# The second weights of all sixteen experts are kept on chip in a vision tower with a mixture of experts

## The chip, the cores and the metric

The kernel runs on one core of one Trainium2 chip. The metric is the device time of a run in microseconds. Three runs of the kernel before gave 906.76, 907.35 and 907.6 us; their median is 907.35 us.

## The reference, cut to what matters

```
tok   = concat(class, patches(x) @ W.T + b) * pos         # 128 images x 65 tokens x 128, x is 128 x 3 x 224 x 224
h     = tok + sigmoid([window_attention(ln(tok)), ln(tok)] @ W_c)
z     = layer_norm(ln(h), g, b)                           # the block's input is ln(h)
gate  = softmax((z @ router_w + router_b) / 0.7)          # 16 experts, the best 2 are kept
ey    = silu(z @ ew1[e] + eb1[e]) @ ew2[e] + eb2[e]       # ew1: 16 x 128 x 512, ew2: 16 x 512 x 128
moe   = sum over the 2 experts of gate * ey  +  0.25 * shared(z)
out   = h + ln(h) + moe + silu(layer_norm(moe) @ ff_w1 + ff_b1) @ ff_w2 + ff_b2
```

All of it is float32. The expert part has 8320 tokens with two experts each, 16640 rows.

## The kernel before, in words

Each engine runs its own program, and semaphores tie them together. There are three stages.

The first stage takes 16 groups of 512 tokens. SP loads images into two halves of one large buffer, `region` (`xb[0]` and `xb[1]`, 14336 columns each), VectorE and ScalarE move them into the patch buffers `xf` and `xlast`, and TensorE multiplies them with the patch weights `wp`; attention, routing and layer norms of the group before are woven in. GpSimd scatters each token's normalised row twice into the DRAM buffer `z_rows`, sorted by expert. In the last group the image loads stop, and SP uses the free halves of `region` for what the next stage needs: the shared expert's weights, tokens of earlier groups (`load_ht`, the first `HT_LOW`, which is 6, at once and six more when `xb[1]` is free), and first and second weights of experts 0 to 3 (`w1b`, `w2b`, lines 485 and 486).

The second stage takes 80 tiles of 256 rows, each of one expert. Tiles 0 to 15 are the first tile of experts 0 to 15; for the others a table `ejc`, made on chip at the end of the first stage, holds the expert's number. The first four tiles and the last five steps are written out, and the rest is a loop of four tiles per turn. A step `j` on TensorE (`step2`) is: transpose tile `j+1` (`t_in`, line 1615), the up-projection of tile `j` (`up`, line 1626: 4 column blocks x 3 terms of split float32, 12 matmuls), and the down-projection of tile `j-1` (`down`, line 1637: 2 row halves x 4 blocks, each matmul run as two passes, 16 in all). ScalarE takes the transpose out of PSUM (line 788) and applies silu (line 798) with the expert's bias, whose address it gets by reading `ejc` into a register (line 794). VectorE splits rows and first weights into high and low parts (lines 1274 to 1279 and 1223 to 1225), and adds the expert's second bias to the down-projection (line 1268). GpSimd scatters the result rows (line 916).

SP feeds this stage. For tile `j` it reads the tile's row into a register and loads the rows (`expert_rows`, line 514), then reads the expert's number and loads 256 KB of first weights (line 506) and 256 KB of second weights (line 508). All three have four buffers in a ring. Every fourth tile it also loads a residual (line 542). The order of these loads is the order of the program. Before the loop SP zeroes the tails of `z_rows` (line 419), loads the first four tiles' rows, the third stage's weights (line 534) and two more token loads (line 475).

The third stage gathers the two results of each token, adds the shared expert, and runs the last feed-forward block.

Of the kernel before, what the change touches and what calls it, by code (L numbers as in the profile page):

```python
# [28 lines left out]
P = 128  # L29
D = 128  # L30
# [5 lines left out]
TILES = PATCH_TILES + 1  # L36
GT = 4
GTOK = GT * P
GIMG = GTOK // SEQ
GROUPS = PATCH_TILES // GT  # L40
TOKENS = TILES * P
E, DH, DS = 16, 512, 256
EC, SC = DH // P, DS // P
TOPK = 2
# [11 lines left out]
MAIN = 21  # L56
# [11 lines left out]
N_LOADS = 18  # L68
FILL, EARLY = 7, 12
SP_TAILS = 12  # L70
assert EARLY % 2 == 0 and EARLY + 4 == GROUPS
# [41 lines left out]
def build(nc, consts, x, tok_w, tok_b, cls_tok, pos, w_c, ln_g, ln_b, r_w, r_b, ew1, eb1, ew2, eb2,  # L113
          sw1, sb1, sw2, sb2, f_g, f_b, fw1, fb1, fw2, fb2, out):
    with ExitStack() as ctx:
        def sb(name, shape, dt=F32):
            return ctx.enter_context(nc.sbuf_tensor(name, shape, dt))

        def sem(name):
            return ctx.enter_context(nc.semaphore(name))  # L120
# [24 lines left out]

        wp = sb("wp", [P, MAIN, D])
        wc = sb("wc", [P, 2, D])
# [11 lines left out]
        XZ = XCOLS // 4  # L159
        region = sb("region", [P, 2 * XCOLS])  # L160
        xb = [region[:, u * XCOLS:(u + 1) * XCOLS] for u in range(2)]
# [6 lines left out]
        def carve(n):  # L168
            carved[0] += n
            assert carved[0] <= 2 * XCOLS  # L170
            return region[:, carved[0] - n:carved[0]]
# [3 lines left out]
        sw2_t = carve(SC * D).rearrange("p (c d) -> p c d", c=SC)  # L175
        ht3 = [carve(GTOK) for _ in range(2)]
        assert carved[0] <= XCOLS
        shared_with_stage3 = carved[0]
        w1b = [carve(W) for _ in range(4)]
        w2b = [carve(W).rearrange("p (c d) -> p c d", c=EC) for _ in range(4)]  # L180
        eh_at = carved[0]
        ehT = [carve(EC * EROWS).rearrange("p (c r) -> p c r", c=EC) for _ in range(2)]
        zin = [carve(EH * ZW).rearrange("p (h d) -> p h d", h=EH) for _ in range(4)]
        h2T = [carve(EROWS) for _ in range(2)]
        yout = [carve(EH * D).rearrange("p (h d) -> p h d", h=EH) for _ in range(2)]
        fw1_t = carve(DH)
        fw2_t = carve(EC * D).rearrange("p (c d) -> p c d", c=EC)
        r_at = carved[0]
        r_res = carve(TILES * D)
        HT_LOW = (XCOLS - r_at) // GTOK  # L190
        sh_res = carve(TILES * D)


        carved[0] = shared_with_stage3
        moe = [carve(GT * D).rearrange("p (t d) -> p t d", t=GT) for _ in range(2)]
        z4 = carve(GT * D).rearrange("p (t d) -> p t d", t=GT)
        h4T = carve(GTOK)
        ffs = carve(EC * GTOK).rearrange("p (c r) -> p c r", c=EC)
        assert carved[0] <= eh_at
        carved[0] = eh_at  # L200
        gat = [carve(GT * TOPK * D).rearrange("p (t k d) -> p t k d", t=GT, k=TOPK) for _ in range(2)]
        assert 2 * GT * TOPK * D <= 2 * EC * EROWS + 4 * EH * ZW + 2 * EROWS + 2 * EH * D

# [4 lines left out]

        xf = sb("xf", [P, QUADS * 4 * HTOK])
        xquad = [xf[:, u * 4 * HTOK:(u + 1) * 4 * HTOK].rearrange("p (q t j) -> p q t j", q=2, j=2) for u in range(QUADS)]  # L210
        xlast = sb("xlast", [P, HTOK])
        eb2_rows = xf[:, 0:E * D]
        shs = [xf[:, E * D + u * SC * GTOK:E * D + (u + 1) * SC * GTOK].rearrange("p (c r) -> p c r", c=SC) for u in range(2)]
        wparts = sb("wparts", [P, 2 * DH + 2 * DS], F32R)
# [116 lines left out]
        w1_loaded = [sem(f"w1_loaded{u}") for u in range(4)]  # L331
        w2_loaded = [sem(f"w2_loaded{u}") for u in range(4)]
        zin_loaded = [sem(f"zin_loaded{u}") for u in range(4)]
# [37 lines left out]
        def one(body, g):  # L371
            body(g, g % 2, g // 2)
# [33 lines left out]
        def units_before(g, u):  # L406

            return g * (HALVES * UNITS) + u * UNITS
# [17 lines left out]
        def _(sp):  # L426
# [52 lines left out]
            for dst, src in ((sw1_t, sw1), (sw2_t, sw2.rearrange("(c p) d -> p c d", p=P)),  # L479
                             (sbq[:, :], sb2.partition_broadcast(P))):  # L480
                sp.dma_start(dst, src).then_inc(sh_loaded, 16)
            for i in range(HT_LOW):
                load_ht(i)
            for j in range(FIRST):
                sp.dma_start(w1b[j], ew1[j]).then_inc(w1_loaded[j], 16)
                sp.dma_start(w2b[j], ew2[j].rearrange("(c p) d -> p c d", p=P)).then_inc(w2_loaded[j], 16)
            one(stores, GROUPS - 3)
            sp.wait_ge(memset_done, 1)

            for s in range(2, SPARE_TILES):  # L490
                at = SPARE_AT + s * EROWS
                sp.dma_start(z_rows[at:at + EROWS].rearrange("(p h) d -> p h d", p=P), zsrc).then_inc(spare_zeroed, 16)
            sp.wait_ge(xact_ready, units_before(GROUPS, 0))
            for i in range(HT_LOW, EARLY):
                load_ht(i)
            one(stores, GROUPS - 2)
            sp.wait_ge(xunit_used, units_before(GROUPS, 0))
# [5 lines left out]
            def expert_weights(j, n):  # L503
                ex = sp.value_load(ejc[0:1, bass.ds(j, 1)], min_val=0, max_val=E - 1)
                sp.wait_ge(w1l_ready, j - 3)
                sp.dma_start(w1b[n % 4], ew1[bass.ds(ex, 1)].rearrange("o d h -> d (o h)")).then_inc(w1_loaded[n % 4], 16)
                sp.wait_ge(down_done, j - 3)
                sp.dma_start(w2b[n % 4], ew2[bass.ds(ex, 1)].rearrange("o (c p) d -> p (o c) d", p=P))\
                  .then_inc(w2_loaded[n % 4], 16)

# [14 lines left out]
            for j in range(FIRST):  # L525
                sp.dma_start(zin[j], z_rows[j * CAP:j * CAP + EROWS].rearrange("(p h) d -> p h d", p=P))\
                  .then_inc(zin_loaded[j], 16)
            zero_tails(sp, FIRST, SP_TAILS)

            sp.wait_ge(r_free, 16 * (GROUPS + 1))  # L530
# [887 lines left out]
        def _(pe):  # L1418
# [210 lines left out]

            def down(j, n, h):  # L1630
                pe.wait_ge(w2_loaded[n % 4], h * 16 + 16)
                if n > 1:
                    pe.wait_ge(yout_ready, j - 1)
                pe.wait_ge(eh_ready, j * EC + EC)
                for i in range(EH):
                    for c in range(EC):
                        ins = pe.matmul(bank[5 + n % 2][:, i * P:(i + 1) * P], ehT[n % 2][:, c, i * P:(i + 1) * P],  # L1637
                                        w2b[n % 4][:, c], start=c == 0, stop=c == EC - 1)
                ins.then_inc(down_done, 1)

            def step2(j, n, h, first=0):

                if not (isinstance(j, int) and j + 1 >= EXPERT_TILES):
                    t_in(j + 1, n + 1, h + (n % 4 + 1) // 4)
                if not (isinstance(j, int) and j >= EXPERT_TILES):
                    up(j, n, h)
                if n - 1 >= first and not (isinstance(j, int) and j > EXPERT_TILES):
                    down(j - 1, n - 1, h - (n % 4 == 0))

            t_in(0, 0, 0)  # L1650
            pe.wait_ge(shr_ready, EARLY)
            for j in range(4):
                step2(j, j, 0)
            with pe.Fori(1, EXPERT_TILES // 4 - 1) as i:
                for n in range(4):
                    step2(i * 4 + n, 4 + n, i)
# [78 lines left out]
```

## Time and profile before

| what | value |
|---|---|
| median of three runs | 907.35 us |
| span of the profiled execution, first to last instruction | 972.0 us |
| first stage, about | 0 to 517 us |
| expert stage, about | 517 to 829 us |
| third stage, about | 829 to 972 us |
| TensorE, weight loads of TensorE, VectorE, ScalarE, GpSimd busy | 92, 82, 70, 62, 45% of the span |
| bytes moved by SP's queue | 166.24 MB |
| mean granted clock of TensorE | 0.975 of full |

The profile is of one execution, with a recording of every instruction and DMA packet. Its span is the only time shown of it, and it is longer than the runs without a recording. PE is TensorE's matmuls, PEld its weight loads, DVE VectorE, ACT ScalarE, POOL GpSimd; SPq is SP's queue, and a name with q (ACTq, PEldq) means instructions that an engine's sequencer handles alone, such as register loads. Stages have different bounds, so the shares over the span say little of any one of them.

### The profile page before, as it was taken

The page shows a single profiled execution, that of the slowest core. Times are in us where ns is not written, and L with a number is a line of the kernel's source. Part 1 is how long each engine was busy: PE and PEld are TensorE (multiplying, and loading weights), DVE is VectorE, ACT ScalarE, POOL GpSimd, SP SyncE. Part 2 cuts the span into 40 slices and gives each one's busy share as a digit, 9 for nine tenths or more (in the row PEclk, how much of TensorE's full clock was granted, in tenths as well). Part 3 has the DMA queues.
Part 4 walks back from the last instruction along what each step waited for, and adds up shares of the span by engine and source line. Part 5 has one row for each costly group of instructions (what it writes and reads, how often), then busy time and mean ns, then how long its engine had stood idle before and what let it go on. Part 6 is the DMA issues. An engine that isn't in the chain of part 4 may idle for free. (4 is left out here: it accounts for less than half of the span.)

```text
span 972.0 us, 22164 instructions
## 1 busy us (share of the span) xinstructions
PE 896.2 (92%) x5920; PEld 801.2 (82%) x5920; DVE 676.2 (70%) x2244; ACT 599.5 (62%) x1064; POOL 438.8 (45%) x374
## 2 busy tenths in 40 slices
PE   2999999989999999999889999999999899789999
PEld 2788888778878888888779889898999899679888
DVE  8377877757877887787556666666676675488884
ACT  3567666656666666777645565555555565477766
POOL 6012554425555545554451445455555464334342
PEclk9999999979999999999879999999999999989999
DMA  9999999977788888767137687777778675334432
GB/s 225 224 221 225 242 247 240 237 205 210 213 228 218 214 216 219 194 216 213 50 105 215 196 227 218 214 219 228 216 224 236 184 221 166 107 82 115 107 103 57
DMA packets 194299, 186.96 MB, mean 192 GB/s; under 512 B 16797, under 2 KB 168698, under 8 KB 194010
## 3 DMA queue, kind: packets, MB, share of 16 engines
q1 hardware_dynamic: 183168, 166.24, 65.2%
q0 software_dynamic: 9376, 19.42, 6.1%
q10 hardware_dynamic: 1722, 0.93, 0.5%
q8 instruction: 12, 0.20, 0.1%
q14 instruction: 21, 0.17, 0.1%
HBM read 150.48 MB, written 36.04 MB: 192 GB/s over the span
## 5 line engine op out<-in xcount | busy, mean ns | idle before, releaser
L1435 PE MATMUL bank<-xf,wp 128*128 128x256 f32 x1280 | 314.0, 394 | 8.4 <-ACT xf L632 5.4
L1435 PEld LDWEIGHTS bank<-xf,wp 128*128 128x128 f32 x1280 | 237.7, 192 | 51.6 <-issue 7.4
L916 POOL DMA_INDIRECT y_tok<-region,dsti x160 | 162.9, 1018 | 164.9 <-DVE region L1268 119.0
L874 POOL TENSOR_TENSOR rstd<-var,neghalf 128x4 f32<-128x4 f32 (+2 forms) x51 | 80.6, 1580 | 287.9 <-DVE var L1030 156.4
L632 ACT ACTIVATE xf<-region 128x1024 f32<-128x1024 f32 x160 | 174.0, 1137 | 18.3 <-DVE region L947 18.3
L890 POOL DMA_INDIRECT z_rows<-z,posg x130 | 157.3, 1210 | 52.5 <-issue 52.2
L798 ACT ACTIVATE region<-bank,cols 128x256 f32<-128x256 f32 x320 | 132.3, 476 | 55.2 <-PE bank L1626 37.2
L1637 PE MATMUL bank<-region 128*128 128x128 f32 x1280 | 156.8, 275 | 1.1 <-DVE region L1268 1.0
L1637 PEld LDWEIGHTS bank<-region 128*128 128x128 f32 x1280 | 150.4, 192 | 1.7 <-issue 1.5
L1626 PE MATMUL bank<-parts 128*128 128x256 f32 x960 | 136.6, 290 | 14.2 <-DVE parts L1279 8.8
L1626 PEld LDWEIGHTS bank<-parts 128*128 128x128 f32 x960 | 119.6, 190 | 25.7 <-issue 19.0
L947 DVE COPY region<-region 32x1792 f32<-32x1792 f32 x96 | 104.8, 1092 | 50.3 <-ACT hT L652 28.9
L788 ACT ACTIVATE region<-bank,cols 128x256 f32<-128x256 f32 x80 | 45.4, 567 | 81.0 <-PE bank L1615 46.5
L1223 DVE CAST parts<-region 128x512 fp32r<-128x512 f32 x80 | 35.4, 443 | 70.9 <-DMA region<-in_L_ffn_ew 56.7
L1684 PE MATMUL bank<-region 128*128 128x128 f32 x520 | 61.7, 277 | 0.0
L1684 PEld LDWEIGHTS bank<-region 128*128 128x128 f32 x520 | 59.4, 192 | 0.9 <-ACT region L819 0.5
L1225 DVE TENSOR_TENSOR parts<-region,parts 128x512 fp32r<-128x512 f32 x80 | 55.6, 694 | 2.8
L1329 DVE SCALAR_TENSOR_TENSOR region<-region,w_all 128x128 f32<-128x128 f32 x130 | 50.3, 446 | 7.6 <-issue 5.3
L1665 PE MATMUL bank<-parts,wparts 128*128 128x512 f32 (+1 forms) x204 | 51.5, 403 | 3.4 <-DVE parts L1368 3.4
L1665 PEld LDWEIGHTS bank<-parts,wparts 128*128 128x128 f32 x204 | 37.5, 195 | 12.0 <-issue 3.6
L834 ACT ACTIVATE region<-region,nmr,rstd 128x128 f32<-128x128 f32 x65 | 26.9, 484 | 30.3 <-DVE nmr L1363 30.3
L819 ACT ACTIVATE region<-bank,cols 128x512 f32<-128x512 f32 (+1 forms) x68 | 40.6, 657 | 3.0 <-PE bank L1665 3.0
(183 smaller groups left out, 1232.3 us busy)
## 6 DMA issues: line engine op xcount, KB each, us to landing
region<-in_x SPq DMA_DIRECT2D x384, 196.0 KB
region<-in_L_ffn_ew SPq DMA_DIRECT2D x160, 256.0 KB
region<-z_rows SPq DMA_DIRECT2D x80, 130.0 KB
region<-y_tok SPq DMA_DIRECT2D x16, 512.0 KB, 3.6
ht_dram<-hT SPq DMA_DIRECT2D x16, 256.0 KB
r_dram<-rr SPq DMA_DIRECT2D x16, 256.0 KB
region<-ht_dram SPq DMA_DIRECT2D x16, 256.0 KB, 5.5
region<-r_dram SPq DMA_DIRECT2D x16, 256.0 KB
```

The lines of the kernel that those rows point to most:

```text
L632: ins = act.activation(xquad[i].rearrange("p q t j -> p t q j"), src[:, :, 4 * i:4 * i + 4].rearrange("p t (q j) -> p t q j", j=2), ACT.Copy)
L798: act.activation(ehT[n % 2][:, c], bank[1 + c][:, 0:EROWS], ACT.Silu, bias=bias[c])\
L874: pool.tensor_tensor(dst, var, neghalf[:, 0:var.shape[1]], ALU.pow).then_inc(ready, 1)
L890: pool.indirect_dma_start(z_rows, bass.IndirectOffsetOnAxis(posg[k][:, n:n + 1], 0), z[k][:, t], None).then_inc(z_free[k], 16)
L916: pool.indirect_dma_start(y_tok, bass.IndirectOffsetOnAxis(dsti[n % 2][:, i:i + 1], 0), yout[n % 2][:, i], None).then_inc(y_free[n % 2], 16)
L947: dve.tensor_copy(dst, src).then_inc(block_moved, 1)
L1225: dve.tensor_tensor(w1l[n % 2], w1b[n % 4], w1h[n % 2], ALU.subtract).then_inc(w1l_ready, 1)
L1435: ins = pe.matmul(out_cols, wp[:, s], cols_in, start=s == 0, stop=s == MAIN - 1)
L1626: ins = pe.matmul(bank[1 + c][:, 0:EROWS], w[n % 2][:, c * P:(c + 1) * P], v[n % 2], start=i == 0, stop=i == len(terms) - 1)
L1637: ins = pe.matmul(bank[5 + n % 2][:, i * P:(i + 1) * P], ehT[n % 2][:, c, i * P:(i + 1) * P], w2b[n % 4][:, c], start=c == 0, stop=c == EC ...
L1665: ins = pe.matmul(dst, w[:, c * P:(c + 1) * P], v[:, 0:nt * P], start=i == 0, stop=i == len(terms) - 1)
L1684: ins = pe.matmul(bank[FFD_BANK[k]][:, t * P:(t + 1) * P], ffs[:, c, t * P:(t + 1) * P], fw2_t[:, c], start=c == 0 and t == 0, stop=c == E ...
```

## The change: what it does

The second weights of all 16 experts get a place of their own in SBUF, `w2all` (16 x 512 columns). They are loaded once: experts 0 to 3 before the last group's end, 4 to 7 when `xb[1]` is free, 8 to 15 after the last table zeroing. SP's loop no longer loads second weights and no longer waits for `down_done`. TensorE reads the expert's number of tile `j-1` into a register in each step, between `t_in` and `up`, and the down-projection addresses `w2all` by that register; for tiles 0 to 15 in the written-out steps the number is known when the program is built. TensorE waits for the three groups of loads by constants. To make room, the patch buffers `xf` and `xlast` and the patch weights `wp` move into one arena with `region`, and the expert stage's smaller buffers move into their part of it. Six token loads (`FIRST_HT` to `EARLY`) no longer wait for `xb[1]`.

```diff
+FIRST_HT = 6
...
-        wp = sb("wp", [P, MAIN, D])
...
-        region = sb("region", [P, 2 * XCOLS])
+        XF, XL, WP = QUADS * 4 * HTOK, HTOK, MAIN * D
+        ARENA = 2 * XCOLS + XF + XL + WP
+        region = sb("region", [P, ARENA])
...
+        r_res = carve(TILES * D)
         assert carved[0] <= XCOLS
-        shared_with_stage3 = carved[0]
+        weights_at = carved[0]
         w1b = [carve(W) for _ in range(4)]
-        w2b = [carve(W).rearrange("p (c d) -> p c d", c=EC) for _ in range(4)]
-        eh_at = carved[0]
+        W2_LOW = (XCOLS - carved[0]) // W
+        w2all = carve(E * W)
+        weights_end = carved[0]
         ehT = [carve(EC * EROWS).rearrange("p (c r) -> p c r", c=EC) for _ in range(2)]
+        h2T = [carve(EROWS) for _ in range(2)]
+        assert carved[0] <= 2 * XCOLS
+        sh_res = carve(TILES * D)
...
+        eb2_rows = carve(E * D)
+        shs = [carve(SC * GTOK).rearrange("p (c r) -> p c r", c=SC) for _ in range(2)]
         zin = [carve(EH * ZW).rearrange("p (h d) -> p h d", h=EH) for _ in range(4)]
...
+        xf = region[:, 2 * XCOLS:2 * XCOLS + XF]
...
-        w2_loaded = [sem(f"w2_loaded{u}") for u in range(4)]
+        w2_low, w2_mid, w2_high = sem("w2_low"), sem("w2_mid"), sem("w2_high")
...
-            for i in range(HT_LOW):
+            def load_w2(lo, hi, done):
+                for e in range(lo, hi):
+                    sp.dma_start(w2all[:, e * W:(e + 1) * W].rearrange("p (c d) -> p c d", c=EC),
+                                 ew2[e].rearrange("(c p) d -> p c d", p=P)).then_inc(done, 16)
+
+            for i in range(FIRST_HT):
                 load_ht(i)
             for j in range(FIRST):
                 sp.dma_start(w1b[j], ew1[j]).then_inc(w1_loaded[j], 16)
-                sp.dma_start(w2b[j], ew2[j].rearrange("(c p) d -> p c d", p=P)).then_inc(w2_loaded[j], 16)
             one(stores, GROUPS - 3)
...
+            for i in range(FIRST_HT, EARLY):
+                load_ht(i)
+            load_w2(0, W2_LOW, w2_low)
+            one(stores, GROUPS - 2)
             sp.wait_ge(xact_ready, units_before(GROUPS, 0))
-            for i in range(HT_LOW, EARLY):
-                load_ht(i)
-            one(stores, GROUPS - 2)
+            load_w2(W2_LOW, 2 * W2_LOW, w2_mid)
             sp.wait_ge(xunit_used, units_before(GROUPS, 0))
...
                 sp.wait_ge(w1l_ready, j - 3)
                 sp.dma_start(w1b[n % 4], ew1[bass.ds(ex, 1)].rearrange("o d h -> d (o h)")).then_inc(w1_loaded[n % 4], 16)
-                sp.wait_ge(down_done, j - 3)
-                sp.dma_start(w2b[n % 4], ew2[bass.ds(ex, 1)].rearrange("o (c p) d -> p (o c) d", p=P))\
-                  .then_inc(w2_loaded[n % 4], 16)
...
             zero_tails(sp, FIRST, SP_TAILS)
+            load_w2(2 * W2_LOW, E, w2_high)
...
-            def down(j, n, h):
-                pe.wait_ge(w2_loaded[n % 4], h * 16 + 16)
+            def down(j, n, ex):
                 if n > 1:
                     pe.wait_ge(yout_ready, j - 1)
                 pe.wait_ge(eh_ready, j * EC + EC)
+                w2 = [w2all[:, bass.ds(ex * W + c * D, D)] for c in range(EC)]
                 for i in range(EH):
                     for c in range(EC):
                         ins = pe.matmul(bank[5 + n % 2][:, i * P:(i + 1) * P], ehT[n % 2][:, c, i * P:(i + 1) * P],
-                                        w2b[n % 4][:, c], start=c == 0, stop=c == EC - 1)
+                                        w2[c], start=c == 0, stop=c == EC - 1)
...
                     t_in(j + 1, n + 1, h + (n % 4 + 1) // 4)
-                if not (isinstance(j, int) and j >= EXPERT_TILES):
+                if n - 1 >= first:
+                    ex = j - 1 if static and j - 1 < E else \
+                        pe.value_load(ejc[0:1, bass.ds(j - 1, 1)], min_val=0, max_val=E - 1)
+                if not (static and j >= EXPERT_TILES):
                     up(j, n, h)
...
             pe.wait_ge(shr_ready, EARLY)
+            pe.wait_ge(w2_low, 16 * W2_LOW)
             for j in range(4):
                 step2(j, j, 0)
+            pe.wait_ge(w2_mid, 16 * W2_LOW)
+            pe.wait_ge(w2_high, 16 * (E - 2 * W2_LOW))
+            pe.wait_ge(tab_ready, 1)
             with pe.Fori(1, EXPERT_TILES // 4 - 1) as i:
```

`W2_LOW` comes out as 4.

## Rows read from the trace of the kernel before

**Rows 1.** The page, part 1: busy us (share) xinstructions of each engine.

```profile
PE 896.2 (92%) x5920; PEld 801.2 (82%) x5920; DVE 676.2 (70%) x2244; ACT 599.5 (62%) x1064; POOL 438.8 (45%) x374
```

**Rows 2.** Weight loads of TensorE in order of time: start, us, count, idle before.

```profile
531.31 1.49 PEld L1626 LDWEIGHTS bank<-parts 128*128 128x128 f32 x12 [0.54 <-issue]
...
823.01 1.50 PEld L1626 LDWEIGHTS bank<-parts 128*128 128x128 f32 x12
```

**Rows 3.** Matmuls of TensorE in order of time, where nothing is late.

```profile
745.95 1.67 PE L1626 MATMUL bank<-parts 128*128 128x256 f32 x12
747.46 1.95 PE L1637 MATMUL bank<-region 128*128 128x128 f32 x16
749.25 0.38 PE L1615 MATMUL bank<-cst,region 128*128 128x128 f32 x2
749.38 1.67 PE L1626 MATMUL bank<-parts 128*128 128x256 f32 x12
```

**Rows 4.** Waits of the expert loop, 531 to 823 us: total, times, longest.

```profile
DVE parts L1223 <- DMA region<-in_L_ffn_ew: 53.9, 42, 3.6
...
PEld bank L1626 <- issue: 19.0, 35, 1.0
...
PE bank L1626 <- DVE parts L1279: 8.5, 26, 0.7
```

**Rows 5.** The same stretch: busy us of each engine, clock, DMA share, GB/s.

```profile
531.30:823.00 291.70, 273.74 (x2247) 259.95 (x2248) 190.71 (x544) 166.19 (x392) 153.18 (x151) 1.00 0.75 214
```

**Rows 6.** What SP itself waited for in that stretch.

```profile
SPq L508 <- remote: 2.2, 4, 1.6
```

**Rows 7.** SP's weight loads: count, ns min/median/max, first and last start.

```profile
L506 SPq DMA_DIRECT2D region<-in_L_ffn_ew x76: 4/318/725, 524.7 to 816.6; - x76
...
L508 SPq DMA_DIRECT2D region<-in_L_ffn_ew x76: 13/396/1010, 525.2 to 817.1; - x76
```

**Rows 8.** SP's queue in order of time, an undisturbed stretch.

```profile
655.16 0.32 SPq L506 DMA_DIRECT2D region<-in_L_ffn_ew  x1
655.58 0.40 SPq L508 DMA_DIRECT2D region<-in_L_ffn_ew  x1
656.92 0.35 SPq L514 DMA_DIRECT2D region<-z_rows  x1
```

**Rows 9.** Register work of ScalarE: count, ns min/median/max, first and last start.

```profile
L794 ACTq FUSED_REGOPS  x152: 42/152/152, 518.8 to 822.0; - x152
L794 ACTq TENSOR_LOAD <-ejc x80: 273/279/497, 518.4 to 821.6; - x80
...
L798 ACTq FUSED_REGOPS  x320: 46/46/51, 519.3 to 826.1; - x160
```

**Rows 10.** Register instructions of TensorE's sequencer at single places (start us).

```profile
L1613 PEldq ALU_OP  x1: 32/32/32, 652.2 to 652.2; - x1
...
L1634 PEldq ALU_OP  x1: 32/32/32, 653.0 to 653.0; - x1
...
L1634 PEldq ALU_OP  x1: 32/32/32, 638.5 to 638.5; - x1
...
L1654 PEldq ALU_OP  x1: 32/32/32, 638.9 to 638.9; - x1
```

**Rows 11.** TensorE's weight loads just after the third of these places.

```profile
653.11 1.49 PEld L1626 LDWEIGHTS bank<-parts 128*128 128x128 f32 x12
```

**Rows 12.** Busy times, clock, DMA share and GB/s, 519 to 531 us.

```profile
519.00:531.00 12.00, 12.00 (x104) 11.71 (x102) 7.80 (x23) 7.86 (x20) 2.11 (x2) 1.00 0.90 256
```

**Rows 13.** Start of the expert loop: SP's queue and VectorE in order of time.

```profile
519.24 0.89 SPq L534 DMA_DIRECT2D region<-in_L_ffn_ff_w  x2
...
524.72 0.35 SPq L506 DMA_DIRECT2D region<-in_L_ffn_ew  x1
...
528.47 0.43 DVE L1223 CAST parts<-region 128x512 fp32r<-128x512 f32 x1 [2.81 <-DMA region<-in_L_ffn_ew]
528.93 0.69 DVE L1225 TENSOR_TENSOR parts<-region,parts 128x512 fp32r<-128x512 f32 x1
```

**Rows 14.** SP's queue in the last group of the first stage.

```profile
449.32 0.50 SPq L498 DMA_DIRECT2D xf<-in_L_ffn_eb  x1
472.67 0.33 SPq L447 DMA_DIRECT2D ht_dram<-hT  x1
```

More of the change, by code:

```diff
@@ L169, in carve @@
             carved[0] += n
-            assert carved[0] <= 2 * XCOLS
+            assert carved[0] <= ARENA
             return region[:, carved[0] - n:carved[0]]
@@ L176, in build @@
         ht3 = [carve(GTOK) for _ in range(2)]
+        r_res = carve(TILES * D)
         assert carved[0] <= XCOLS
-        shared_with_stage3 = carved[0]
+        weights_at = carved[0]
         w1b = [carve(W) for _ in range(4)]
-        w2b = [carve(W).rearrange("p (c d) -> p c d", c=EC) for _ in range(4)]
-        eh_at = carved[0]
+        W2_LOW = (XCOLS - carved[0]) // W
+        w2all = carve(E * W)
+        weights_end = carved[0]
         ehT = [carve(EC * EROWS).rearrange("p (c r) -> p c r", c=EC) for _ in range(2)]
+        h2T = [carve(EROWS) for _ in range(2)]
+        assert carved[0] <= 2 * XCOLS
+        sh_res = carve(TILES * D)
+        assert carved[0] >= 2 * XCOLS
+        eb2_rows = carve(E * D)
+        shs = [carve(SC * GTOK).rearrange("p (c r) -> p c r", c=SC) for _ in range(2)]
         zin = [carve(EH * ZW).rearrange("p (h d) -> p h d", h=EH) for _ in range(4)]
-        h2T = [carve(EROWS) for _ in range(2)]
         yout = [carve(EH * D).rearrange("p (h d) -> p h d", h=EH) for _ in range(2)]
[L186 to L194, printed above, removed]
+        fw1_t = sb("fw1_t", [P, DH])[:, :]
+        fw2_t = sb("fw2_t", [P, EC * D])[:, :].rearrange("p (c d) -> p c d", c=EC)
+        carved[0] = weights_at
         moe = [carve(GT * D).rearrange("p (t d) -> p t d", t=GT) for _ in range(2)]
@@ L198, in build @@
         ffs = carve(EC * GTOK).rearrange("p (c r) -> p c r", c=EC)
-        assert carved[0] <= eh_at
-        carved[0] = eh_at
         gat = [carve(GT * TOPK * D).rearrange("p (t k d) -> p t k d", t=GT, k=TOPK) for _ in range(2)]
-        assert 2 * GT * TOPK * D <= 2 * EC * EROWS + 4 * EH * ZW + 2 * EROWS + 2 * EH * D
+        assert carved[0] <= weights_end
         parts = sb("parts", [P, 4 * W + 4 * EROWS], F32R)
@@ L207, in build @@
         h2h, h2l = ([parts[:, 4 * W + (2 * c + u) * EROWS:4 * W + (2 * c + u + 1) * EROWS] for u in range(2)] for c in range(2))
-        xf = sb("xf", [P, QUADS * 4 * HTOK])
+        xf = region[:, 2 * XCOLS:2 * XCOLS + XF]
         xquad = [xf[:, u * 4 * HTOK:(u + 1) * 4 * HTOK].rearrange("p (q t j) -> p q t j", q=2, j=2) for u in range(QUADS)]
-        xlast = sb("xlast", [P, HTOK])
-        eb2_rows = xf[:, 0:E * D]
-        shs = [xf[:, E * D + u * SC * GTOK:E * D + (u + 1) * SC * GTOK].rearrange("p (c r) -> p c r", c=SC) for u in range(2)]
+        xlast = region[:, 2 * XCOLS + XF:2 * XCOLS + XF + XL]
+        wp = region[:, 2 * XCOLS + XF + XL:ARENA].rearrange("p (s h) -> p s h", s=MAIN)
         wparts = sb("wparts", [P, 2 * DH + 2 * DS], F32R)
@@ L1637, in down @@
                         ins = pe.matmul(bank[5 + n % 2][:, i * P:(i + 1) * P], ehT[n % 2][:, c, i * P:(i + 1) * P],
-                                        w2b[n % 4][:, c], start=c == 0, stop=c == EC - 1)
+                                        w2[c], start=c == 0, stop=c == EC - 1)
                 ins.then_inc(down_done, 1)
             def step2(j, n, h, first=0):
-                if not (isinstance(j, int) and j + 1 >= EXPERT_TILES):
+                static = isinstance(j, int)
+                if not (static and j + 1 >= EXPERT_TILES):
                     t_in(j + 1, n + 1, h + (n % 4 + 1) // 4)
-                if not (isinstance(j, int) and j >= EXPERT_TILES):
+                if n - 1 >= first:
+                    ex = j - 1 if static and j - 1 < E else \
+                        pe.value_load(ejc[0:1, bass.ds(j - 1, 1)], min_val=0, max_val=E - 1)
+                if not (static and j >= EXPERT_TILES):
                     up(j, n, h)
-                if n - 1 >= first and not (isinstance(j, int) and j > EXPERT_TILES):
-                    down(j - 1, n - 1, h - (n % 4 == 0))
+                if n - 1 >= first:
+                    down(j - 1, n - 1, ex)
             t_in(0, 0, 0)
             pe.wait_ge(shr_ready, EARLY)
+            pe.wait_ge(w2_low, 16 * W2_LOW)
             for j in range(4):
                 step2(j, j, 0)
+            pe.wait_ge(w2_mid, 16 * W2_LOW)
+            pe.wait_ge(w2_high, 16 * (E - 2 * W2_LOW))
+            pe.wait_ge(tab_ready, 1)
             with pe.Fori(1, EXPERT_TILES // 4 - 1) as i:
```

## The prediction

> **What bounds the kernel now.** I read the busy shares first, then the stretches, then the waits of the one stretch that the change enters, and last single queues in order of time. TensorE is busy 896.2 us of the 972.0 us span [rows 1], so a gain must come from a place where TensorE itself waits. The change enters the expert stage. Its steady part runs from the first weight load of tile 4's up-projection (531.31) to that of tile 79 (823.01) [rows 2]: 291.70 us for 75 tiles, 3.889 us each. When nothing is late, a tile takes less: the up-projections at 745.95 and 749.38 stand 3.43 us apart [rows 3]. 75 x 3.43 = 257.3 us, so 34.4 us of the stage is TensorE waiting, in slices of under a microsecond.
>
> For what? TensorE's waits sit in front of the up-projection: 19.0 us put down to issue and 8.5 us to VectorE's low halves of the rows [rows 4]. VectorE has only 190.71 us of work in the 291.70, 2.54 us a tile [rows 5], but it waits 53.9 us for a DMA that brings first weights [rows 4]. That DMA is issued by SP, and SP waits for nobody: the longest of its waits in the stage sums to 2.2 us [rows 6]. It issues 76 first-weight loads from 524.7 to 816.6, that is 291.9 / 75 = 3.89 us per tile [rows 7], the stage's own pace. So the stage runs at the rate at which SP issues: two loads of a register from SBUF, address arithmetic and three DMAs per tile, a fourth every fourth tile. The DMA engines are not full (share 0.75) [rows 5]. ScalarE (2.22 us a tile) and GpSimd (2.04) have room [rows 5].
>
> **The change part by part.**
>
> *Second weights leave SP's loop.* Per tile one DMA of 256 KB and its setup go. In an undisturbed stretch SP starts a first-weight load at 655.16, the second-weight load at 655.58 and the next rows load at 656.92 [rows 8]; the second-weight DMA itself holds SP 0.396 us (median) and about 0.1 us lies ahead of it [rows 7, 8], so 0.5 us goes. If nothing else on SP changed, it would need 3.89 - 0.50 = 3.39 us a tile. That is just under TensorE's 3.43, so TensorE becomes the bound with SP close behind. The bound from the other side: SP's instructions show stalls of 0.7 us (maxima of 725 and 1010 ns beside medians of 318 and 396) [rows 7]; with a third of its DMAs gone, and those the ones cut into 512-byte pieces, some stalls should go too. SP's wait for down_done goes as well, worth little, since it cost 2.2 us in all. I take 3.48 us a tile: the 3.43 floor plus 0.05 for jitter between two nearly equal engines. Gain 75 x (3.889 - 3.48) = 30.7 us; ends 75 x (3.889 - 3.43) = 34.4 and, with SP's uneven iterations still felt at 3.60, 21.7.
>
> *TensorE loads the expert's number and addresses the weights by register.* No such operation of TensorE is in this trace. The nearest row is ScalarE's same load: 279 ns, then 152 ns of register work [rows 9]; with a check behind them and the gaps I estimate 0.7 us. Four products and up to eight address computations, at ScalarE's 46 ns for one [rows 9], make 0.55 us, 1.0 us with gaps nearly as long again. So 1.7 us more per tile on TensorE's sequencer. It is hidden if the sequencer runs ahead of the array. It does: at 653.0 it is past the whole up-projection (it computes the wait of the down-projection), and the array starts that up-projection only at 653.11 [rows 10, 11]. It is thus at least 12 matmuls, 1.41 us, ahead, more than the 0.7 us of the load. Its own time per tile, where nothing holds it: 652.2 to 653.0 for transposes and up-projection, 638.5 to 638.9 for the down-projection [rows 10], 1.2 us. With 1.7 more it is 2.9 us, below 3.43. I take zero; if the cover were gone, 0.7 to 1.7 us a tile. Queued behind the load are the up-projection and all that follows it.
>
> *Eight second-weight loads now stand in SP's order after the last table zeroing and before the first loop loads.* They cost SP 8 x 0.5 = 4.0 us, and 8 x 256 KB at the 256 GB/s of 519 to 531 [rows 12] is 8.2 us of DMA in a stretch that is already 0.90 busy. Behind them wait the third-stage weights (at 519.24), two token loads, the residual load, and tile 4's rows and first weights (issued at 524.72, split by VectorE from 528.47, after 2.81 us of waiting) [rows 13]. Tile 4 therefore lands 4.0 to 8.2 us later; I take 6. Of that, some 1.4 us is slack: the split of 0.43 and 0.69 us ends at 529.6 while tile 4's up-projection starts at 531.31 [rows 2, 13]. So it costs 4.6 us (2.6 to 6.8), once; later tiles can't win it back from an array at its floor. TensorE's wait for these loads (it stands ahead of the loop and holds all behind it) ends about when they land, near 528, and costs no more than the same delay.
>
> *Loads in the first stage's last groups.* Experts 0 to 3 replace the four loads of before, a little later; experts 4 to 7 are 1 MB more near 447. Both are needed only after 523. SP sits idle from its load at 449.32 to 472.67 [rows 14], waiting for ScalarE. The six token loads and one store that move ahead of a wait go the same way. The bias rows behind them are first used in the expert stage, 70 us on. Cost nothing; without that cover 4 x 0.5 = 2 us. The wait for experts 0 to 3 is past long before the stage. New places in SBUF for patch buffers and weights change no instruction's size: nothing, from rows that stay as they are.
>
> **Sum.** On the profiled execution -30.7 + 4.6 = -26 us: a span of about 946 us. Only that execution's span is shown, and the timed runs' median is 907.35 us, 64.65 us less. Where the recording costs that time no row says. If it is spread evenly, the gain is 26 x 907.35 / 972.0 = 24 us; if SP and the DMAs bear more of it than TensorE, the timed runs have less idle time to give back. Half of the 34.4 us gone would leave 17 - 4.6 = 12 us. I take 19 us: **888 us**, 876 to 899 for this case.
>
> **The rivals.**
>
> *TensorE's sequencer becomes the bound (the other side).* Place: the down-projection, whose 16 passes per tile carry a register address. Without one, the 16 go out in 0.4 us [rows 10]. If each pass pays address work of its own (16 x 0.1 us instead of 8) and goes out more slowly by as much again, 2.9 us becomes 5.3; at half of that increase it is 4.1. It costs time from 3.89 us a tile on; at 4.1 it is 75 x 0.21 + 4.6 = 20 us slower in the profile, about 926 us timed. For it: TensorE shows no instruction of this form. Against it: 0.5 us of margin before there is a loss of gain, 1.0 us before there is a loss of time.
>
> The Trainium skill, "TensorE: Matmul & The Clock Gate", Part 1 ("Wait — 56ns, not 53.3ns?"), speaks for this rival: it says that matmuls are decoded in hardware and bypass the sequencer's microcode, and that with that decoding off the microcode spends about 62 ns on each. The quick plain passes agree with its first half; whether a register address costs a matmul this path it does not say, and no run here shows it. By that page's figure 16 passes would add an estimated 1.0 us: 3.9 us a tile, no gain, the late start lost, about 911 us. I count this inside the rival's chance.
>
> *The feeder stays the bound.* Rows, first weights and residual keep SP at 3.55 to 3.6 us a tile, and the late start costs all of 6.8 us: 75 x 0.30 - 6.8 = 16 us in the profile, some 9 timed, 898 us. For it: the longest gaps come at SP's loop ends, which stay. Against it: four buffers for rows and for first weights.
>
> *The loop's idle time exists only under the profiler.* Then the timed runs gain a few us and lose the start: 903 to 908. For it: 64.65 us is unexplained. Against it: SP's path is a chain of register loads and DMA issues which no recording explains away.
>
> *It doesn't do what it says:* second weights would be read from a wrong expert or arrive late. Waits on constants guard each group of loads, so I give this nothing.
>
> **How the numbers follow.** Forecast (876 to 899) 0.64; even better 0.04; feeder stays (893 to 903) 0.12; idle only under the profiler 0.08; sequencer bound 0.12 (no change a quarter of it, slower the rest). The range for 8 in 10 runs from 875 to 908. What a measurement can tell from no change is 0.2%, 1.8 us. Faster: 0.64 + 0.04 + 0.11 + 0.02 = 0.81; same: 0.01 + 0.05 + 0.03 = 0.09; slower: 0.01 + 0.09 = 0.10.
>
> **What would show it.** Right: up-projections 3.43 to 3.5 us apart all through the loop, VectorE's wait for first weights gone, SP waiting for VectorE in the loop, DMA share about 0.5, and tile 4 starting near 536. Wrong: a new idle time of TensorE in front of the up-projection after its own register load (sequencer), or VectorE still waiting for first weights with SP never waiting (feeder). A first gap at tile 4 of 8 us or more would mean that I mis-sized the late start.

## The result, and the profile after

The changed kernel takes 917.41 us (median of 4, 916.07 to 919.09), the kernel before 907.48 us on the same chip (4 runs): a ratio of 1.0112, 95% interval 1.0098 to 1.0126. It is slower by 10 us; the forecast was 888.0 us, faster. Of all executions timed for this document one, of the version with four late loads, took 4965 us; it is left out of that version's ratio.

What the prediction expected of the expert loop is all there. The page of the changed kernel, part 1 (busy us, share, instructions), answers to [rows 1]:

```profile
PE 869.1 (95%) x5920; PEld 792.2 (87%) x5921; DVE 678.4 (74%) x2244; ACT 595.5 (65%) x1064; POOL 439.0 (48%) x374
```

Its weight loads in order of time (start, us, engine, line, operation, count, idle before in brackets) answer to [rows 2]; L1633 is the up-projection, L1622 the transposes of the next tile's rows, L1644 the down-projection. The fence has the up-projection of tile 2, then tile 3 with the transposes of tile 4's rows ahead of it, then tiles 4 and 79:

```profile
495.45 1.49 PEld L1633 LDWEIGHTS bank<-parts 128*128 128x128 f32 x12
...
506.66 0.29 PEld L1622 LDWEIGHTS bank<-cst,region 128*128 128x128 f32 x2 [7.92 <-DMA region<-z_rows]
506.93 2.68 PEld L1633 LDWEIGHTS bank<-parts 128*128 128x128 f32 x12
509.50 3.12 PEld L1644 LDWEIGHTS bank<-region 128*128 128x128 f32 x16
512.54 0.26 PEld L1622 LDWEIGHTS bank<-cst,region 128*128 128x128 f32 x2
512.76 0.42 PEld L1633 LDWEIGHTS bank<-parts 128*128 128x128 f32 x3
...
770.04 1.50 PEld L1633 LDWEIGHTS bank<-parts 128*128 128x128 f32 x12
```

From tile 4 (512.76) to tile 79 (770.04) it is 257.28 us for 75 tiles, 3.430 us each: the floor of [rows 3]. The stretch as a whole (busy us of PE, PEld, DVE, ACT, POOL, then clock, DMA share, GB/s) answers to [rows 5], and what SP waited for in it to [rows 6]:

```profile
512.70:770.00 257.30, 257.30 (x2251) 257.30 (x2249) 191.57 (x542) 161.40 (x392) 153.72 (x150) 1.00 0.56 165
```
```profile
SPq L520 <- DVE dstf L1282: 49.9, 53, 1.4
```

TensorE is busy all the time, the DMA share fell to 0.56, and SP now waits 49.9 us for VectorE: it runs ahead. Yet the span is 914.9 us, and this profiled execution was timed at 916.7 us, so the recording as such did not lengthen it. The 972.0 us execution of the kernel before, on which the prediction rests, was an unusually long one, some 65 us over the timed runs; the second profile of that kernel, below, confirms it.

The loss stands in the first fence: 7.92 us of idle time ahead of tile 3, and then one tile at half speed (weight loads 2.68 and 3.12 us, where the rows of an undisturbed tile show 1.49 and 1.88). SP's queue just before it answers to [rows 13] (start, us, line, target, count):

```profile
486.21 5.43 SPq L421 DMA_DIRECT2D z_rows<-zeros  x8
491.68 5.52 SPq L487 DMA_DIRECT2D region<-in_L_ffn_ew  x8
497.30 1.18 SPq L541 DMA_DIRECT2D fw_t<-in_L_ffn_ff_w  x2
498.53 1.37 SPq L541 DMA_DIRECT2D fbq<-in_L_ffn_ff_b  x1
499.94 0.97 SPq L477 DMA_DIRECT2D region<-ht_dram  x2
501.46 0.37 SPq L549 DMA_DIRECT2D region<-r_dram  x1
502.76 0.37 SPq L520 DMA_DIRECT2D region<-z_rows  x1
```

The eight late loads (L487) hold SP for 5.52 us. Tile 4's rows (the last line) are issued behind them at 502.76, and TensorE's next transposes can start only at 506.66.

### The profile page after: what moved, and what is told of

Its sections match the earlier page's. It is cut to its first block and busy times, and to the rows that moved or that the text cites. A ratio compares the mean times of both kernels' runs of the same rounds, so it can differ in the third digit from the quotient of the medians.

```text
span 914.9 us, 22563 instructions
## 1 busy us (share of the span) xinstructions
PE 869.1 (95%) x5920; PEld 792.2 (87%) x5921; DVE 678.4 (74%) x2244; ACT 595.5 (65%) x1064; POOL 439.0 (48%) x374
## 5 line engine op out<-in xcount | busy, mean ns | idle before, releaser
L1442 PE MATMUL bank<-region 128*128 128x256 f32 x1344 | 323.0, 391 | 5.4 <-ACT region L639 5.4
L1442 PEld LDWEIGHTS bank<-region 128*128 128x128 f32 x1344 | 247.3, 190 | 51.1 <-issue 4.1
L639 ACT ACTIVATE region<-region 128x1024 f32<-128x1024 f32 x160 | 173.7, 1134 | 17.0 <-DVE region L954 17.0
L1644 PE MATMUL bank<-region 128*128 (+1 forms) x1280 | 156.9, 276 | 0.0
L1644 PEld LDWEIGHTS bank<-region 128*128 128x128 f32 x1280 | 151.2, 193 | 0.0
L805 ACT ACTIVATE region<-bank,cols 128x256 f32<-128x256 f32 x320 | 125.7, 475 | 21.1 <-PE bank L1633 20.6
L1633 PE MATMUL bank<-parts 128*128 128x256 f32 x960 | 135.1, 290 | 0.4 <-DVE parts L1286 0.4
L1633 PEld LDWEIGHTS bank<-parts 128*128 128x128 f32 x960 | 120.4, 191 | 0.7 <-DVE parts L1286 0.6
L795 ACT ACTIVATE region<-bank,cols 128x256 f32<-128x256 f32 x80 | 45.1, 564 | 93.2 <-PE bank L1622 93.2
L1699 PE MATMUL bank<-fw_t,region 128*128 128x128 f32 x520 | 61.7, 277 | 0.0
L1699 PEld LDWEIGHTS bank<-fw_t,region 128*128 128x128 f32 x520 | 59.4, 192 | 1.0 <-ACT region L826 0.5
L1275 DVE TENSOR_TENSOR region<-bank,region 128x256 f32<-128x256 f32 x80 | 34.0, 425 | 25.6 <-PE bank L1644 23.5
L1230 DVE CAST parts<-region 128x512 fp32r<-128x512 f32 x80 | 33.9, 424 | 14.6 <-DMA region<-in_L_ffn_ew 10.1
```

The source lines that it names most:

```text
L639: ins = act.activation(xquad[i].rearrange("p q t j -> p t q j"), src[:, :, 4 * i:4 * i + 4].rearrange("p t (q j) -> p t q j", j=2), ACT.Copy)
L805: act.activation(ehT[n % 2][:, c], bank[1 + c][:, 0:EROWS], ACT.Silu, bias=bias[c])\
L1442: ins = pe.matmul(out_cols, wp[:, s], cols_in, start=s == 0, stop=s == MAIN - 1)
L1633: ins = pe.matmul(bank[1 + c][:, 0:EROWS], w[n % 2][:, c * P:(c + 1) * P], v[n % 2], start=i == 0, stop=i == len(terms) - 1)
L1699: ins = pe.matmul(bank[FFD_BANK[k]][:, t * P:(t + 1) * P], ffs[:, c, t * P:(t + 1) * P], fw2_t[:, c], start=c == 0 and t == 0, stop=c == E ...
```

## Experiments

The experiments ran on three chips, each beside new runs of the kernel before on its own chip (medians 906.8 to 908.1 us). The ratios are to those runs, and different experiments are compared by their ratios.

The theories, by the names that the expectations use. A: the loop of before has nothing to give back in an ordinary execution, and the late loads cost the time (A1 by SP's issue time, A2 by their bytes). B: the loop does stall, and the loss is elsewhere. C: the register address costs. D: the earlier loads in the first stage cost.

**A second profile of the kernel before.** No edit.

> The kernel before, unchanged, for a second profile. Theory A (the profiled execution of before, span 972.0 us against 907.4 timed, was not like the timed ones, and the loop has nothing to give back): span about 905, TensorE's busy time about 865, tiles 4 to 79 about 3.43 us apart instead of 3.89, TensorE's idle time in the loop a few us instead of 17. Theory B (the loop of before does stall in every execution, and the changed kernel loses its time elsewhere): tiles about 3.7 us apart in a span of about 905.

Timed 906.56 us, span 904.7. Its expert loop, the same columns as in [rows 5], and the times of SP's first-weight loads as in [rows 7]:

```profile
502.40:760.20 257.80, 257.74 (x2249) 257.37 (x2248) 190.92 (x545) 161.40 (x392) 153.11 (x152) 1.00 0.83 242
```
```profile
L506 SPq FUSED_REGOPS  x76: 42/42/42, 495.5 to 752.5; - x76
...
L506 SPq DMA_DIRECT2D region<-in_L_ffn_ew x76: 350/351/359, 495.7 to 752.7; - x76
```

TensorE is idle 0.06 us of 257.80, where [rows 5] have 18 of 291.70; tile 4 starts at 502.46, tile 79 at 760.24, 3.437 us a tile. SP's issue takes 350 to 359 ns every time, where [rows 7] have 4, 318 and 725. VectorE still waits for first weights and SP waits too, both hidden behind TensorE:

```profile
DVE parts L1223 <- DMA region<-in_L_ffn_ew: 34.9, 45, 1.9
```
```profile
SPq L508 <- PE bank L1637: 13.4, 32, 0.6
```

B is out for this execution. What had stretched the first one is not known, but it was not the loop alone: tile 0 starts at 518.69 us there and at 488.07 here, 30.6 us apart, and the loop is 33.9 us longer. The start of the loop, against the first fence of the changed kernel:

```profile
493.24 1.49 PEld L1626 LDWEIGHTS bank<-parts 128*128 128x128 f32 x12
...
498.71 0.20 PEld L1615 LDWEIGHTS bank<-cst,region 128*128 128x128 f32 x2 [2.17 <-DMA region<-z_rows]
498.88 1.49 PEld L1626 LDWEIGHTS bank<-parts 128*128 128x128 f32 x12
500.29 1.88 PEld L1637 LDWEIGHTS bank<-region 128*128 128x128 f32 x16
502.08 0.26 PEld L1615 LDWEIGHTS bank<-cst,region 128*128 128x128 f32 x2
502.46 0.66 PEld L1626 LDWEIGHTS bank<-parts 128*128 128x128 f32 x5
```

Tile 4's rows are late in the kernel before too, by 2.17 us, but the array comes back at full speed. SP's queue there, against the one of the changed kernel:

```profile
484.69 5.42 SPq L419 DMA_DIRECT2D z_rows<-zeros  x8
490.21 0.89 SPq L534 DMA_DIRECT2D region<-in_L_ffn_ff_w  x2
...
494.45 0.37 SPq L514 DMA_DIRECT2D region<-z_rows  x1
```

**The loads gone from the loop, and nothing else.**

```diff
-                sp.wait_ge(down_done, j - 3)
-                sp.dma_start(w2b[n % 4], ew2[bass.ds(ex, 1)].rearrange("o (c p) d -> p (o c) d", p=P))\
-                  .then_inc(w2_loaded[n % 4], 16)
...
-                pe.wait_ge(w2_loaded[n % 4], h * 16 + 16)
+                pe.wait_ge(w2_loaded[n % 4], 16)
```

> The kernel before, without the 76 loads of second weights in the loop and without the waits for them: every tile's down-projection reads the weights of the first four experts, so the output is not the reference's. It does alone what the prediction took for the gain. Theory A: 907 (906 to 908), the loop had no idle time to give back. Theory B: about 888, as the prediction had it.

906.47 us, ratio 0.9995 (0.9983 to 1.0006). This is the gain of the prediction's main step, taken by itself: nothing, in timed runs. In its profile TensorE is busy for all of the same stretch, with the DMA share at 0.57:

```profile
502.40:760.20 257.80, 257.80 (x2255) 257.80 (x2254) 191.82 (x544) 161.34 (x393) 155.64 (x152) 1.00 0.57 166
```

**All second weights early.**

```diff
             load_w2(W2_LOW, 2 * W2_LOW, w2_mid)
+            load_w2(2 * W2_LOW, E, w2_high)
...
             zero_tails(sp, FIRST, SP_TAILS)
-            load_w2(2 * W2_LOW, E, w2_high)
```

> The changed kernel, with the eight late loads of second weights (experts 8 to 15) issued behind those of experts 4 to 7, before the last stores of stage 1, and no longer between the tails and the first rows of the loop. Theory A (the eight late loads, 5.5 us of SP's time, delay tile 4's rows and leave TensorE at half clock): 907 us (905 to 909), the gap between tiles 2 and 3 shrinks from 11.5 to under 6 us. Theory C (the register address on TensorE costs the time): 917, the late loads were hidden. Theory D (the loads in the filled stage delay it): 917 or more, because eight more now stand there.

908.37 us, ratio 1.0009 (0.9992 to 1.0026). The loss is gone, with the register address and everything else of the change in place; C and D don't hold, to within the interval. SP's queue in the last group of stage 1 answers to [rows 14]:

```profile
426.60 10.80 SPq L487 DMA_DIRECT2D region<-in_L_ffn_ew  x12
437.44 0.75 SPq L508 DMA_DIRECT2D region<-in_L_ffn_eb  x1
448.31 0.34 SPq L449 DMA_DIRECT2D ht_dram<-hT  x1
```

Twelve loads take 10.80 us there, and SP is still idle from 438.2 to 448.3. At the start of the loop TensorE has no wait for rows.

**Fixed addresses.**

```diff
-                    ex = j - 1 if static and j - 1 < E else \
-                        pe.value_load(ejc[0:1, bass.ds(j - 1, 1)], min_val=0, max_val=E - 1)
+                    ex = j - 1 if static and j - 1 < E else n % 4
```

> The changed kernel with fixed addresses in the down-projection of tiles 4 to 79 (second weights of experts 0 to 3 in turn, so the output is not the reference's) and no register load on TensorE. Theory A: 917 (916 to 918), the address costs nothing. Theory C: 907 or less, 0.13 us for each of 76 tiles comes back.

915.85 us, ratio 1.0099 (1.0084 to 1.0113), beside 1.0112 (1.0098 to 1.0126) with the register. Tiles 4 and 79 stand 257.28 us apart in both traces. C is out.

**The late loads alone, in the kernel before.** Five go to the patch weights' old place, three to columns of the residual buffer that are filled much later. SP, too, waits for them, at the end of each turn of its loop.

```diff
             zero_tails(sp, FIRST, SP_TAILS)
+            for e in range(2 * FIRST, E):
...
+                sp.dma_start(dst, ew2[e].rearrange("(c p) d -> p c d", p=P)).then_inc(extra_loaded, 16)
...
+                sp.wait_ge(extra_loaded, 16 * (E - 2 * FIRST))
...
+            pe.wait_ge(extra_loaded, 16 * (E - 2 * FIRST))
             with pe.Fori(1, EXPERT_TILES // 4 - 1) as i:
```

> The kernel before with nothing of the change but eight extra loads of 256 KB on SP's queue where the changed kernel has its late ones (into places that nothing reads; TensorE waits for them ahead of its loop, as it does in the changed kernel). Theory A: 916 to 918, the whole loss without layout, register address or earlier loads. If something else of the change shares the loss, 908 to 914.

914.66 us, ratio 1.0066 (1.0049 to 1.0082). The eight loads alone bring about six tenths of the loss, less than I expected. TensorE's wait for tile 4's rows is as long as in the changed kernel; the first line is this run's, the second the changed kernel's:

```profile
PE bank L1622 <- DMA region<-z_rows: 8.1, 1, 8.1
...
PE bank L1622 <- DMA region<-z_rows: 7.7, 1, 7.7
```

Tile 4 follows tile 3 in 4.74 us, not 5.83, so the half-clock stretch was 1.1 us shorter. The rest of the difference, 2 to 3 us of timed runs, stays open.

**Half as many late loads.** Experts 8 to 11 early, 12 to 15 late.

> The changed kernel with four of the eight late loads moved to the early place, four left late. Theory A1 (0.69 us of SP for each late load, all of it on the path once some 2 us of cover are used up, and half clock behind a long wait): 910 to 913, TensorE waits 4 to 6 us for tile 4's rows in place of 7.7. Were the loss one of having any late load at all, 917.

913.29 us, ratio 1.0053 (1.0035 to 1.0071). TensorE's wait:

```profile
PE bank L1622 <- DMA region<-z_rows: 5.9, 1, 5.9
```

None, four and eight late loads give 0, 5.9 and 7.7 us of waiting, and 1.0009, 1.0053 and 1.0112: the loss grows with the number.

**Issue time or bytes.** First, on the version with fixed addresses (ratio 1.0099), an eighth of the bytes in as many pieces:

```diff
-            load_w2(2 * W2_LOW, E, w2_high)
+            for e in range(2 * W2_LOW, E):
+                sp.dma_start(w2all[:, e * W:(e + 1) * W].rearrange("p (c d) -> p c d", c=EC)[:, :, 0:16],
+                             ew2[e].rearrange("(c p) d -> p c d", p=P)[:, :, 0:16]).then_inc(w2_high, 16)
```

> The changed kernel with fixed addresses in the loop as in the run before (its time was 915.9) and the eight late loads cut to an eighth of their bytes, 64 bytes in place of 512 in each of as many descriptors (the output is not the reference's). Theory A1 (the loss is the 5.5 us that SP needs to issue eight loads, with everything behind them on its queue): 914 to 917. Theory A2 (the loss is the time of 2.1 MB on the DMA engines, some 10 us at the 200 GB/s of this stretch): 907 to 909.

913.66 us, ratio 1.0068 (1.005 to 1.0086). Some 2 to 3 us came back with seven eighths of the bytes; two thirds of the loss stayed. SP's queue:

```profile
490.24 4.39 SPq L536 DMA_DIRECT2D region<-in_L_ffn_ew  x8
494.73 2.06 SPq L543 DMA_DIRECT2D fw_t<-in_L_ffn_ff_w  x2
...
500.16 0.37 SPq L520 DMA_DIRECT2D region<-z_rows  x1
```

Eight loads that carry little are still issued in 4.39 us, where the run with fixed addresses and whole loads has 5.20. So mostly A1: the queue is held by something other than the bytes, and the bytes add to it. Whether it is the instructions or their pieces this run doesn't tell. Second, the same 2.1 MB as one instruction:

```diff
-            load_w2(2 * W2_LOW, E, w2_high)
+            sp.dma_start(w2all[:, 2 * W2_LOW * W:].rearrange("p (c d) -> p c d", d=D),
+                         ew2[2 * W2_LOW:E].rearrange("e (c p) d -> p (e c) d", p=P)).then_inc(w2_high, 16)
```

> The changed kernel with the eight late loads made one instruction of 2.1 MB at the same place. Theory A2: 917, the bytes are the same. Theory A1: if one instruction is issued in some 0.7 us, 908 to 910; if its issue takes as long as the eight (it has as many descriptors), 917, and this run tells nothing.

917.43 us, ratio 1.0096 (1.0079 to 1.0113): no gain, though the instruction itself takes 0.88 us:

```profile
492.88 0.88 SPq L535 DMA_DIRECT2D region<-in_L_ffn_ew  x1
493.87 5.83 SPq L542 DMA_DIRECT2D fw_t<-in_L_ffn_ff_w  x2
499.74 0.55 SPq L542 DMA_DIRECT2D fbq<-in_L_ffn_ff_b  x1
500.34 1.93 SPq L477 DMA_DIRECT2D region<-ht_dram  x2
...
504.15 0.37 SPq L520 DMA_DIRECT2D region<-z_rows  x1
```

The time shows in the two loads behind it (5.83 us, 0.89 in the second profile of before). By its time this run can't tell A1 from A2, since 917 had been expected under both. The trace adds that the issue itself is short and that tile 4's rows still leave no earlier, 11.3 us behind the start of the large load and 11.1 us behind that of the eight. Fewer instructions don't help, since the wait is handed to the next ones. With the run before, that leaves the number of pieces as the likely cause; no run varied it alone.

**The same loads on the same queue, later.** Tiles 8 to 15 use experts 8 to 15 in order, so each load can stand behind its own tile's rows and first weights; the first passes of SP's and TensorE's loops are written out for it, and TensorE waits for each load ahead of the product that reads it.

```diff
-            load_w2(2 * W2_LOW, E, w2_high)
...
                 for n in range(4):
                     expert_loads(j, 4 + n)
+                    if isinstance(i, int) and j >= 2 * W2_LOW:
+                        load_w2(j, j + 1, w2_high)
```

> The changed kernel with the same eight late loads on the same queue, but each issued behind the rows and first weights of its own tile (tiles 8 to 15 use experts 8 to 15 in that order), as the kernel before loads them; from tile 16 on none. TensorE waits for each ahead of its down-projection. Theory A1 (it is the place on SP's queue, ahead of tile 4's rows): 907 (906 to 909), and tile 3 starts 3.4 to 5.6 us behind tile 2. Theory C (something in the kept weights or the register address costs it): 916.

909.92 us, ratio 1.0021 (1.0001 to 1.0041): about 8 us of the loss gone, a little over the range that A1 gave. Tile 3 starts 5.23 us behind tile 2, with a wait of 1.6 us for rows, much as in the kernel before (2.0). Moved earlier or later, the same loads cost little or nothing: the place is what costs.

**Towards a better version.** With all weights early, the rows and first weights of tile 4 go ahead of stage 3's weights:

```diff
+            sp.wait_ge(tails_zeroed, 16 * (E - FIRST))
+            sp.wait_ge(dstf_ready, 1)
+            sp.dma_start(zin[0], z_rows[FIRST * CAP:FIRST * CAP + EROWS].rearrange("(p h) d -> p h d", p=P))\
+              .then_inc(zin_loaded[0], 16)
+            sp.wait_ge(w1l_ready, 1)
+            sp.dma_start(w1b[0], ew1[FIRST]).then_inc(w1_loaded[0], 16)
             sp.wait_ge(r_free, 16 * (GROUPS + 1))
...
+            loop_loads(1, 1)
+            with sp.Fori(2, 1 + GROUPS) as i:
```

> All second weights early (the run that came to 908.4 against 907.2 of before), and the rows and first weights of tile 4 issued ahead of stage 3's weights instead of behind them. In the second profile of before VectorE waits 4.58 us for those first weights, and tile 3 starts 5.64 us behind tile 2 instead of 3.43. Theory A (what is queued on SP ahead of tile 4 sets the start of the loop): 2 us less than that run, 905 to 907. If the loop's start is set by something else: 908.

909.01 us, ratio 1.001 (0.9994 to 1.0026): no gain. Tile 5's rows now came later, and TensorE waited for those:

```profile
504.01 0.43 PE L1630 MATMUL bank<-cst,region 128*128 128x128 f32 x2 [1.97 <-DMA region<-z_rows]
505.30 1.88 PE L1641 MATMUL bank<-parts 128*128 128x256 f32 x12 [0.85 <-issue]
506.98 3.41 PE L1652 MATMUL bank<-region 128*128 x16
```

The down-projection behind these two gaps, the last line, takes 3.41 us, where [rows 3] have 1.95.

Next come tiles 4 and 5 together (the same edit in a loop over two tiles):

> All second weights early, and the rows and first weights of tiles 4 and 5 both issued ahead of stage 3's weights, the shared expert's last rows and the first residual. With only tile 4's ahead, tile 5's came later than without (498.06 against 494.47 + 2.47 = 496.94 us) and TensorE waited 1.97 us for them. Theory A1: no wait of TensorE for rows in the first tiles, 905.5 to 907.5. Else 908 to 909.

906.48 us, ratio 0.998 (0.9965 to 0.9995), and no wait for rows. TensorE has another wait instead, ahead of tile 5's up-projection and for VectorE:

```profile
507.80 1.69 PE L1643 MATMUL bank<-parts 128*128 128x256 f32 x12 [1.33 <-DVE parts L1296]
```

It is the one complete version under both kernels, by 0.2%, as much as a measurement can tell. Is that the order alone? The same order in the kernel before, second weights in the loop as they were:

> The kernel before, its second weights in the loop as they were, with the order of the run that came to 0.998 of before: rows and first weights of tiles 4 and 5 ahead of stage 3's weights, the shared expert's last rows and the first residual (the second weights of these two tiles behind them). Theory A1 (the start of the loop is set by the order on SP, and the kept weights bring nothing): 906 to 907, 0.2 per cent under before. If that run's gain came from the kept weights: 908, as before.

907.65 us, ratio 1.0006 (0.9986 to 1.0025). The order alone shows no gain there, and TensorE waits 1.3 us for tile 6's rows. The two intervals overlap between 0.9986 and 0.9995, so whether the kept weights have a share in the 0.2% stays open.

## Why the prediction was wrong

*What bounds the kernel.* "34.4 us of the stage is TensorE waiting" failed, and with it the forecast. It was true of the one execution recorded, and the timed runs don't have it: the second profile shows 0.06 us, and taking the loads away brought nothing. Nor did SP set the stage's pace, as I had it: in the second profile SP waits 13.4 us for TensorE's down-projections. The sum was made in an execution 64.65 us longer than the timed median. I scaled the gain down to 19 us and left the question whether it exists to a rival. Two signs stood in my own rows: SP's issue times of 4 to 725 ns for 76 equal loads [rows 7], and a tile at 3.43 us wherever one looked at an undisturbed place [rows 3]; 75 x (3.889 - 3.43) = 34.4 us is half of the 64.65 us that had no explanation.

*Second weights leave SP's loop.* SP's loop did get lighter (it waits 49.9 us, 13.4 before), and the tile time is 3.430 us (I took 3.48). It was worth nothing, since 3.437 was there before and SP was not the bound.

*The register address.* Right: hidden, zero. The Trainium skill, "TensorE: Matmul & The Clock Gate", Part 1, says nothing on whether a product with a register address keeps the fast path. The runs with and without the address show the same 257.28 us for 75 tiles.

*Loads in the first stage.* Right within the noise, even for twelve (1.0009).

*Eight late loads.* The sign was right and the size too small: 4.6 us (2.6 to 6.8) forecast, some 8 us in the trace and 10 timed. In the two traces (changed against the second profile of before) tile 0 starts 2.21 us later (490.28 and 488.07), the step from tile 2 to tile 3 grows by 5.84 us (11.48 and 5.64), that from tile 3 to tile 4 by 2.25 (5.83 and 3.58), the loop shrinks by 0.50, the rest grows by 0.40: 10.2 us, the difference of the spans. The first term is not the change's: over the second profile of before and those of all experiments tile 0 starts between 488.07 and 491.47. Nearly all of it is the clock at the end of the first stage. From the same product of that stage (at 450.93 and 450.65) to tile 0 it is 39.35 and 37.42 us, at a granted clock of 0.83 and 0.94 from 460 to 490 us. The kernel before without its loop loads has 39.41 us at 0.84, the changed kernel with fixed addresses 37.40 at 0.94.

Of the rest the sum missed two terms. I had taken 6 us of delay, and the step from tile 2 to tile 3 did grow by 5.84, but I had deducted 1.4 us of slack where TensorE already waited 2 us for these rows. And I had no term for the restart at half clock, 2.25 us. SP's part of the delay, 4.0 us by my count, was too small as well: from the end of the table zeroing to the issue of tile 4's rows SP takes 11.1 us, 4.3 in the second profile of before. Of the 6.8 more, 5.6 are the loads and 1.2 the instructions behind them. I had also looked at the wrong reader: not the first weights of tile 4 decide, but its rows, which TensorE transposes ahead of tile 3's up-projection and behind which tile 3 queues.

*The rivals.* "The loop's idle time exists only under the profiler" came nearest, at a chance of 0.08, and its 903 to 908 us was short by the mis-sized late start. The name was wrong: recording doesn't stretch a run in general (914.9 us of span beside 916.7 timed, and 904.7 beside 906.56 for the kernel before). Sequencer and feeder were both wrong. The sign named in advance, a first gap of 8 us or more, is what came: 11.48 us, at tile 3.

## What to carry to other kernels

A gain read from a profile is worth what the timed runs have of it. Where the profiled execution is 7% longer than the timed ones, look first for the rows that can't belong to an ordinary run (equal instructions with scattered times), and count the stall that you mean to remove as possibly part of the excess; a second profile settles it. Before a bulk load goes into an in-order queue, list what stands behind it: the price is not the load but the first late row, the engine that waits for it, and the slow tile after the wait; put the load where the queue is idle or where its data is needed, not at a seam.

## What the runs showed of the hardware

After 7.92 us without work TensorE came back at the lower of its two clock levels (1.2 GHz), after 2.17 us at the upper one (2.4 GHz). The granted clock (third figure from the end) of the changed kernel from tile 3's transposes to tile 4, and of the second profile of before around the same place:

```profile
506.60:512.70 6.10, 6.03 (x31) 6.04 (x32) 3.56 (x10) 2.55 (x6) 1.96 (x2) 0.55 0.59 161
```
```profile
484.00:512.00 28.00, 24.90 (x212) 24.09 (x212) 18.90 (x53) 15.47 (x37) 8.46 (x9) 1.00 0.77 227
```

The wait for rows thus cost 2.2 us more than its length. A short gap isn't safe by itself: in the run with tile 4's rows ahead, gaps of 1.97 and 0.85 us with 0.43 us of work between them were followed by a down-projection of 3.41 us in place of 1.95.

The time that one large load takes on SP's queue appears at the instructions behind it: 0.88 us for 2.1 MB, then 5.83 us for two loads that take 0.89 us elsewhere. The Trainium skill, "Perfetto Trace Analysis", section "Per-instruction lifecycle", says that the window of such a DMA in the profile holds its wait for the descriptor generator and ends before the data has moved. The second part agrees: 2.1 MB in 0.88 us would be some 2400 GB/s, where the stretches shown here have 161 to 256. What holds the two loads behind it for 5.83 us no row shows.
